# Expert rows in units of 256 instead of 128, with w1 blocks as the stationary operand and gathers three units ahead

## The reference

```python
x = x + attention(layernorm(x), ctx, ctx)      # 16 heads of 16, 154 keys per batch
h = layernorm(x)
top2 = top_k(softmax(h @ router_w.T), 2)       # 8 experts
for e in range(8):
    w   = sum of the token's top2 weights that name e
    out = out + w * (gelu(h @ w1[e].T, exact) @ w2[e].T)   # 256 -> 1024 -> 256
return x + out
```

## Time and profile before

| | us |
|---|---|
| median of 3 runs (505.07 to 507.56) | 507.27 |
| profiled execution, its own time | 507.12 |
| its span in the profile | 505.3 |

### The profile page before, as it was taken

How to read it: one execution, slowest core, us unless ns; L and a number is a source line. 1 busy time by engine, 2 the same in 40 slices (tenths; PEclk the granted TensorE clock), 3 DMA queues, 4 the chain that set the end, 5 groups by cost and what they waited for, 6 DMA issues and landing times.

```text
span 505.3 us, 12174 instructions
## 1 busy us (share of the span) xinstructions
PE 446.7 (88%) x3485; PEld 390.4 (77%) x3486; DVE 332.8 (66%) x792; ACT 233.6 (46%) x403; POOL 250.7 (50%) x301
## 2 busy tenths in 40 slices
PE   7778999999999997227599999999999999999980
PEld 4567888888888885113489999999999889999970
DVE  3678999999999995697357374564436667433440
ACT  2465676766676764220435353442335544333220
POOL 2788877778877775105034244443333436333431
PEclk9799999999999999558979999999999999999986
DMA  8401121111111110601454526244222653222220
GB/s 244 153 0 54 57 81 54 62 52 62 59 76 52 64 53 32 188 2 52 167 188 70 183 44 205 45 127 105 39 42 42 197 198 46 37 42 42 43 35 10
DMA packets 23083, 41.72 MB, mean 83 GB/s; under 512 B 5808, under 2 KB 18736, under 8 KB 22032
## 3 DMA queue, kind: packets, MB, share of 16 engines
q1 hardware_dynamic: 12512, 28.67, 15.9%
q0 software_dynamic: 7056, 9.88, 11.5%
q10 hardware_dynamic: 3488, 2.83, 1.8%
HBM read 25.88 MB, written 9.19 MB: 69 GB/s over the span
## 4 chain that ended last, share of the span: by engine, by line
PE 73%; DVE 8%; DMA 6%; issue 4%; POOL 3%; ACT 2%; ACTq 1%; DVEq 0%; POOLq 0%; SPq 0%
PE ps_s L1223 18%; PE ps_s L1210 17%; PE ps_s L1057 10%; PE ps_t L1240 6%; PE ps_t L1072 6%; DMA big<-in_wexp 3%; PE ps_a L1090 3%; PE ps_c L1107 3%; PE ps_a L1013 2%; PE ps_a L1085 2%; DMA xs<-in_x 2%; PE ps_c L1194 2%; ACT KB L576 2%; PE ps_c L1119 1%; PE ps_c L1113 1%
## 5 line engine op out<-in xcount | busy, mean ns | idle before, releaser
L448 POOL DMA_INDIRECT result<-big,rowtok x36 | 57.1, 1587 | 149.7 <-issue 63.8
L1223 PEld LDWEIGHTS ps_s<-KB,hidT 128*128 128x128 f32 x864 | 108.2, 190 | 5.8 <-issue 2.8
L1210 PE MATMUL ps_s<-KB,xgT 128*128 (+1 forms) x432 | 110.9, 406 | 0.6 <-issue 0.6
L1223 PE MATMUL ps_s<-KB,hidT 128*128 x864 | 109.5, 282 | 2.1 <-issue 2.1
L1210 PEld LDWEIGHTS ps_s<-KB,xgT 128*128 128x128 f32 x432 | 79.6, 191 | 17.5 <-issue 0.8
L602 ACT ACTIVATE hidT<-ps_t 128x512 fp32r<-128x512 f32 x72 | 39.1, 596 | 91.0 <-PE ps_t L1240 91.0
L1057 PE MATMUL ps_s<-KB 128*128 (+1 forms) x384 | 72.2, 324 | 9.6 <-DVE V_all L695 3.2
L584 ACT ACTIVATE big<-ps_s 128x1024 f32<-128x1024 f32 x36 | 36.9, 1026 | 69.1 <-PE ps_s L1210 68.2
L966 DVE TENSOR_TENSOR hidT<-ps_t,hidT 128x512 fp32r<-128x512 f32 x72 | 46.4, 686 | 33.6 <-ACT hidT L602 32.2
L1057 PEld LDWEIGHTS ps_s<-KB 128*128 128x128 f32 x384 | 57.1, 194 | 14.4 <-issue 7.6
L981 DVE TENSOR_SCALAR big<-ps_s,wrow 128x256 f32<-128x256 f32 x36 | 17.4, 483 | 73.3 <-PE ps_s L1223 73.2
(11 more groups left out here) (160 smaller groups left out, 596.3 us busy)
## 6 DMA issues: line engine op xcount, KB each, us to landing
big<-in_wexp SPq DMA_DIRECT2D x8, 2048.0 KB, 7.9
V_cur<-V_all SPq DMA_DIRECT2D x16, 384.0 KB, 2.6
result<-x SPq DMA_DIRECT2D x16, 128.0 KB, 1.7
rows<-xn SPq DMA_DIRECT2D x16, 128.0 KB, 2.1
xs<-in_x ACTq DMA_DIRECT2D x1, 1536.0 KB, 10.8
big<-rows,gtok POOLq DMA_INDIRECT x39
result<-big,rowtok POOLq DMA_INDIRECT x36
big<-in_ctxT SPq DMA_DIRECT2D x1, 308.0 KB, 3.8
```

The costliest lines, as they stand in the source:

```text
L448: pool.indirect_dma_start(out, bass.IndirectOffsetOnAxis(rowtok[:, u:u + 1], 0), ys[:, u % 2, :], None, compute_op=ALU.add).then_inc(added ...
L1210: last = mm(ps_s[0][:, c, :], xgT[:, u % 2, a, k, :], w1[:, bass.ds(par, 1), w, k, 512 * c:512 * (c + 1)].squeeze(1), start=k == 0 and n = ...
L1223: last = mm(ps_s[1][:, u % 2, 0:D], hidT[:, a, j, :], w2[:, bass.ds(par, 1), w, j, :].squeeze(1), start=j == 0 and n == 0, stop=j == HJ - ...
```

## The change

Experts' lists are padded to units (pairs) of 256 rows, at most `PAIRS` = 23, which are two half-units of 128 for gathers and scatters (`SLOTS` is now 46). `up` holds 128x128 blocks of w1 in the array and streams 256 rows, so the hidden layer comes out turned already: the turns L1240 are gone, and `turn` on VectorE makes both its parts from the GELU's output in SBUF. `down` streams high and low part of w2 side by side (512 columns) against the high part of the hidden layer and 256 columns against its low part; the low product lands in the second half of the bank, is scaled on ScalarE (`scale_low`) and added on VectorE. The split w1 is held once, the split w2 twice; they load as two transfers of 1 MB. Gathers go three units ahead, one in front of each of a unit's two scatters. Tests for used units are nested. The two split tables are replaced by four operations in `first_tables`.

```diff
-SLOTS = (2 * TOK + E * (P - 1)) // P
+PAIR = 2 * P
+PAIRS = (2 * TOK + E * (PAIR - 1)) // PAIR
+SLOTS = 2 * PAIRS
@@ ff_pairs
-            for s in range(FF_LOOP, SLOTS):
+            def remaining(s):
                 with if_used(eng, s):
-                    slot(s, s % 4, s // 4, lambda d, s=s: s + d < SLOTS)
+                    pair(s, s % 4, s // 4, lambda d: s + d < PAIRS)
+                    if s + 1 < PAIRS:
+                        remaining(s + 1)
+                    eng.nop()
+            remaining(FF_LOOP)
@@ sync, expert e
-                    sp.wait_ge(w_lo, HALVES * e)
-                sp.dma_start(wraw, wexp[e]).then_inc(w_loaded, 16)
+                    sp.wait_ge(w1_lo, NP1 * e)
+                sp.dma_start(wraw1, wexp[e, :, 0:W1]).then_inc(w1_loaded, 16)
+                if e:
+                    sp.wait_ge(w2_lo, e)
+                sp.dma_start(wraw2, wexp[e, :, W1:WB]).then_inc(w2_loaded, 16)
@@ gpsimd (left_by(s) waits for gtok_made s+2, xgT_made s+1, wrow_made s+1)
+            def pair(s, u, i, has):
+                if has(3):
+                    left_by(s + 1)
+                for h in range(2):
+                    if has(3):
+                        gather((u + 3) % 4, h)
+                    wait_alone(ys_made, 2 * s + h + 1)
+                    if h or not isinstance(s, int) or s >= 1:
+                        wait_alone(added, 32 * s + 16 * h)
+                    pool.indirect_dma_start(out, bass.IndirectOffsetOnAxis(rowtok[:, u, h:h + 1], 0),
+                                            ys[:, 2 * (u % 2) + h, :], None, compute_op=ALU.add).then_inc(added, 16)
                 if isinstance(s, int) and s >= FF_LOOP:
-                    pool.wait_ge(added, 16 * (s + 1))
+                    pool.wait_ge(added, 32 * (s + 1))
@@ scalar
+            def gelu(s):
+                for b in range(4):
+                    act.wait_ge(up_psum, 4 * s + b + 1)
...
+                    act.activation(hid[:, b, :], ps_s[b // 2][:, b % 2, :], ACT.Gelu).then_inc(hid_made, 1)
+            def scale_low(s, u, h):
+                act.wait_ge(down_psum, 2 * s + h + 1)
...
+                act.activation(y_low[:, h, :], ps_t[h][:, D:2 * D], ACT.Copy,
+                               scale=wrow[:, u, h, 3:4]).then_inc(low_made, 1)
+            def pair(s, u, i, has):
+                if has(1):
...
+                    with act.If(to_split >= E):
+                        split_w2(e, e % 2)
+                    with if_used(act, s + 1):
+                        gelu(s + 1)
+                    with act.If(to_split % E > 0):
+                        split_w1(to_split % E)
+                for h in range(2):
+                    scale_low(s, u, h)
@@ vector
+            def turn(s, u):
...
+                for b in range(4):
+                    js = slice(2 * b, 2 * b + 2)
+                    src = hid[:, b, :].rearrange("p (j n) -> p j n", j=2)
+                    dve.wait_ge(hid_made, 4 * s + b + 1)
+                    dve.tensor_copy(hidT[u % 2][:, 0, js, :], src).then_inc(hidT_hi, 1)
+                    dve.wait_ge(hidT_hi, 4 * s + b + 1)
+                    dve.tensor_tensor(hidT[u % 2][:, 1, js, :], src, hidT[u % 2][:, 0, js, :].bitcast(fp32),
+                                      ALU.subtract).then_inc(hidT_lo, 1)
             take_rows(0, 0, True)
             take_rows(1, 1, True)
-            split_tables_2()
-            split_weights(0, 0, 1)
+            split_w2(0, 0)
...
+            turn(0, 0)
+            with dve.If(to_split > 0):
+                split_w1(to_split % E)
+            def pair(s, u, i, has):
...        # as on scalar: split_w2, turn(s + 1), split_w1
+                if has(2):
+                    take_rows(s + 2, (u + 2) % 4, has(4))
+                for h in range(2):
+                    dve.wait_ge(low_made, 2 * s + h + 1)
+                    if not isinstance(s, int) or s >= 2:
+                        dve.wait_ge(added, 32 * (s - 2) + 16 * (h + 1))
+                    dve.scalar_tensor_tensor(ys[:, 2 * (u % 2) + h, :], ps_t[h][:, 0:D], wrow[:, u, h, 3:4],
+                                             y_low[:, h, :], ALU.mult, ALU.add).then_inc(ys_made, 1)
@@ tensor
+            def up(s, u, e):
+                pe.wait_ge(xgT_made, s + 1)
+                for j in range(HJ):
+                    if j % 4 == 0:
+                        pe.wait_ge(w1_lo, NP1 * e + 2 * (j // 4) + 2)
...
+                    for k in range(KC):
+                        for n, (a, w) in enumerate(PARTS):
+                            last = mm(ps_s[j // 4][:, j // 2 % 2, (j % 2) * PAIR:(j % 2 + 1) * PAIR],
+                                      w1[:, w, k, j * P:(j + 1) * P], xgT[:, u % 2, a, k, :],
...
+            def down(s, u, e):
...
+                for h in range(2):
...
+                    for j in range(HJ):
+                        if h == 0 and j % 2 == 0:
+                            pe.wait_ge(hidT_lo, 4 * s + j // 2 + 1)
+                        mm(ps_t[h][:, :].rearrange("p (w d) -> p w d", w=2), hidT[u % 2][:, 0, j, half_rows],
+                           w2[:, bass.ds(par, 1), :, j, :].squeeze(1), start=j == 0, stop=j == HJ - 1,
...
+                        last = mm(ps_t[h][:, 0:D], hidT[u % 2][:, 1, j, half_rows],
+                                  w2[:, bass.ds(par, 1), 0, j, :].squeeze(1), start=False, stop=j == HJ - 1,
...
             row_transposes(0, 0)
-            row_transposes(1, 1)
             pe.wait_ge(pairs_made, 1)
             read_used(pe)
             up(0, 0, 0)
+            row_transposes(1, 1)
+            def pair(s, u, i, has):
...
+                if has(1):
+                    with if_used(pe, s + 1):
+                        up(s + 1, (u + 1) % 4, e1)
+                if has(2):
+                    row_transposes(s + 2, (u + 2) % 4)
+                down(s, u, e0)
```

More of the change, by code:

```diff
@@ L589, in _ @@
             act.activation(r_e2[:, 0:1], lane_sb[:, :], ACT.Gelu)
+            split_w2(0, 0)
             act.wait_ge(pairs_made, 1)
             read_used(act)
+            to_split = act.value_load(table(t_split, 0), min_val=0, max_val=E * E - 1)
             gelu(0)
-            act.wait_ge(tables_made, 1)
-            def slot(s, u, i, has):
+            with act.If(to_split > 0):
+                split_w1(to_split % E)
+            def pair(s, u, i, has):
                 if has(1):
[L597 to L610, removed]
-                            split_weights(e, e % 2, 1)
@@ L616, in _ @@
+            ff_pairs(act, pair)
         @block.vector
@@ L929, in _, with columns @@
-            split_tables_1()
-            def column(a, s):
-                return a[:, s:s + 1] if isinstance(s, int) else a[:, bass.ds(s, 1)]
+            then(dve.tensor_scalar(t_k[:, :, 0], code, 0.0, None, ALU.is_gt))
+            then(dve.tensor_scalar(t_k[:, :, 1], code, 0.0, None, ALU.is_lt))
+            split_w1(0)
+            def columns(a, s):
+                return a[:, 2 * s:2 * s + 2] if isinstance(s, int) else a[:, bass.ds(2 * s, 2)]
             def take_rows(s, u, more):
@@ L988, in _ @@
+            ff_pairs(dve, pair)
         @block.tensor
@@ L1204, in up @@
                 pe.wait_ge(xgT_made, s + 1)
[L1205 to L1207 removed]
+                for j in range(HJ):
+                    if j % 4 == 0:
+                        pe.wait_ge(w1_lo, NP1 * e + 2 * (j // 4) + 2)
+                    if j % 2 == 0 and (not isinstance(s, int) or s >= 1):
+                        pe.wait_ge(hid_made, 4 * s + j // 2 - 3)
                     for k in range(KC):
@@ L1233, in _ @@
             up(0, 0, 0)
-            def slot(s, u, i, has):
-                pair = pe.value_load(table(t_pair, s), min_val=0, max_val=E * E - 1)
-                e0, e1 = pair % E, pair // E
-                pe.wait_ge(hid_made, s + 1)
-                for j in range(HJ):
-                    last = pe.transpose(ps_t[j // 4][:, (j % 4) * P:(j % 4 + 1) * P], hid[:, j * P:(j + 1) * P],
-                                        id_sb[:, :])
-                last.then_inc(hidT_psum, 1)
-                if has(2):
-                    row_transposes(s + 2, (u + 2) % 4)
+            row_transposes(1, 1)
+            def pair(s, u, i, has):
+                both = pe.value_load(table(t_pair, s), min_val=0, max_val=E * E - 1)
+                e0, e1 = both % E, both // E
                 if has(1):
```

304 lines of the change are left out of this document (141 added, 163 removed).

## The result

| | before | changed |
|---|---|---|
| median of 10 runs, us | 506.25 (505.07 to 507.67) | 503.38 (499.91 to 506.35) |
| profiled execution, us | 507.12 | 504.29 |
| its span, us | 505.3 | 502.1 |
| start of up(0) to end of the last down, us | 257.8 | 251.8 |
| start of the last scatter to the end of the span, us | 11.0 | 8.0 |

The ratio is 0.9935, 95% interval 0.9911 to 0.9959: 0.65% faster. 494.5 us had been forecast. The direction was right and the mechanism on TensorE too; three quarters of the gain were missing. All times and ratios are of executions in the chip's usual state; one execution each of the kernels of experiments 9 and 10 was in a slower one (623.87 and 558.91 us) and is not counted.

What follows compares the result with a forecast made beforehand. TensorE was taken to bound the expert stage: pair 0 ends at 268.1, the rest adds 205.3, then 5 for short experts and 4.6 at the end give 483.0; with the tail, 494.5 us, range 488 to 501.

Steps and rivals of the forecast that it cites:

- TensorE per unit: Expert stage: up 5.66, down 5.62 and row turns 0.44 make 11.72 us per unit, against 13.44 for two slots.
- Rival D: TensorE pays 0.190 us for each w1 block in up: +66 us, 560 in all; chance 0.02.
- Units: The experts' lists make 19 units of 256 rows, 38 half-units against 36 slots; padding costs 5.6%.
- The start: VectorE's work in series is late after up(0): up(1) starts near 254.3, pair 0 ends near 268.1.
- VectorE at the short experts: Pairs 10 and 11: 13.8 us of VectorE work, 2.0 too much, and late w1 reloads; 5 us taken.
- The step that failed: GpSimd: two scatters take 9.5 of 11.7 us a unit, hidden; a late one is caught up.
- rival B: Scatters become the bound through GpSimd's chain, from a period of 5.86 us; at 6.5, 517 us; chance 0.09.
- The end: Last down near 483.0; scatter (18,1) may start at 486.3 and lands near 491.
- The skip: Before the last down, skipping up(19) costs a pause of 2.1 us; 2.8 taken because of a gather.
- The credit for nested tests: After the last landing, one skip of 2.1 us (bounds 0 and 6.2) replaces three unused slots' 6.2 us.
- The sum: Span 493 with the 1.8 us around it: 494.5 us, 12.6 less than the profiled run.
- The range: The forecast's own range is 488 to 501 us; 8 in 10 lie in 484 to 508.

Runs made afterwards that it cites:

- experiments 9 and 10: 9: experiment 1, experiment 4 and experiment 5 together, 489.35 us, ratio 0.9650; 10: that plus the hidden layer's cast on ScalarE, 486.87 us, ratio 0.9630.
- experiment 7: Changed kernel with the number of used units one higher, so a 20th unit of padding is worked through: 515.08 us, ratio 1.0170 to the kernel before.
- experiment 4: Changed kernel with VectorE doing split_w2(0) and turn(0) before take_rows(1) at the start: 499.08 us, ratio 0.9835 to the kernel before.
- experiment 1: Changed kernel with both gathers of a unit issued ahead of both scatters: 497.21 us, ratio 0.9783 to the kernel before.
- experiment 2: Changed kernel with each gather moved below its scatter: 604.14 us, ratio 1.195 to the kernel before.
- experiment 5: Changed kernel with gathers, row turns and making of rows' parts skipped for unused units from unit 16 on: 501.23 us, ratio 0.9879 to the kernel before.
- experiment 6: Changed kernel with the tests for used units flat again instead of nested: 503.68 us, ratio 0.9908 to the kernel before.

## Why the prediction was wrong

- **TensorE per unit** was right: 11.60 us for 11.72. Rival D (a price for each new w1 block) is excluded by the row of 5.62 us for 48 products.
- **Units** were right: 38 scatters; a unit costs 11.9 us (experiment 7).
- **The start** was right in order and size: up(1) at 253.2 (254.3 forecast), pair 0's end at 267.8 (268.1). Only up(0) did not pay for the clock, 5.87 us, and other executions of like kernels did, 7.4. That its idle time was what to fill, experiment 4 showed.
- **VectorE at the short experts** was right in size: 2.0 us too much a pair forecast; a pause of 1.4 us in the changed kernel, 2.15 once the gathers were out of the way, 0.36 with the casts elsewhere. Pairs 10 and 11 cost 8.5 us over two undisturbed units, however (up(11) to up(13), 374.6 to 406.4), and 5 had been taken: 4.11 of them are the next point, and 1.9 the lower clock behind it.
- **The step that failed** is this sentence on the scatters: "the gathers stand three units ahead and the results have four buffers, so a late one is caught up". I had asked whether two scatters of 4.75 us fit in a unit, and they do. I had not asked what stands behind a scatter that waits for its results. The gather of rows for three units on is issued behind the first scatter, which in a slow pair starts only when VectorE is through with splits, hidden layer and rows. "Three units ahead" says which rows it fetches, not how long before their use: 391.90 to 398.46 is no slack at all, and it met the second thing that the sentence passes over: beside a weight load a gather too is slow, 6.52 us for 2.8 to 3.1. Experiment 1 took the gathers from behind the scatter, and the slow landing was then hidden; it got 1.5% back, 7.7 us of the 8.9 missing (no run kept the order and moved the load); experiment 2 closed the ring for both gathers and lost 20%. The rival B named GpSimd's chain, but with a wrong price and threshold: a period of scatters over 5.86 us never was the question.
- **The end**: last down at 489.2, 483.0 forecast; 5.7 us of that come from the middle. The pause ahead of the last down was 3.67 (2.8 forecast): the gather that it waited for was issued at 478.77, behind the scatter of 476.88, and the gather before that at 475.60, when the scatter of 469.40 had landed. The last scatter started 4.9 us behind the last down, 3.3 had been forecast. The difference is the distance of the last two, 6.3 us where 4.75 had been taken. A gather for a unit that doesn't exist stands between them, and without it they are 4.6 us apart (experiment 5). But 476.88 and 481.50 have a gather between them too and are 4.6 apart, so the gather alone doesn't explain it, and the cause of the slow landing (5.48 us for 3.8) is open.
- **The skip** was wrongly read. I took the 2.1 us before the last down of the kernel before for the price of skipping an up. They are a wait for the hidden layer: its rounded copy and its remainder are made while the next up runs, and where there is no next up TensorE waits for them (L1223 is down; compare).

```profile
486.62 1.08 ACT L602 ACTIVATE hidT<-ps_t 128x512 fp32r<-128x512 f32 x2 [2.68 <-PE ps_t L1240]
487.25 1.29 DVE L966 TENSOR_TENSOR hidT<-ps_t,hidT 128x512 fp32r<-128x512 f32 x2 [1.02 <-ACT hidT L602]
...
488.89 4.63 PE L1223 MATMUL ps_s<-KB,hidT 128*128 x24 [2.10 <-issue]
```

  The remainder is ready at 488.5, and 0.35 us are left for the skip and all else. The changed kernel paused at this place too, 3.67 us, but for a gather; without that gather (experiment 5) it doesn't pause. That a pause of 2.8 had been forecast there was luck.
- **The credit for nested tests** was wrong for the same reason. The 6.2 us between the last landing and the end before were not three skips: GpSimd's drain alone takes 6.20 of them there. The end did get 3 us shorter, as forecast, but by luck: 2.6 of the 3.0 are the drain, 3.63 us in the changed kernel, and experiment 6 shows that nesting gives 0.6 at most. By the same run the rule of the Trainium skill ("Runtime: NRT & Kernel Launch", § Instruction fetch mechanics) is not borne out here as a price of 2.1 us for each skip.
- **The sum** came out a little low: (18,1) at 486.3, 4.75 to land, 2.1 and 1.8 give about 494.9, not 494.5.
- **The range**: 484 to 508 held the time, in its upper part; the forecast's own, 488 to 501, did not. The forecast took every pause but one as independent of the others. Two of the pauses (short experts, last down) and the six small ones had one cause in common, a gather behind a scatter.

What stays open: what sets GpSimd's drain. The time from the last scatter to the end is 7.9 to 8.6 us in the kernels whose last gather stands at most 10.2 us ahead of the drain (drain 3.6 to 4.1 us), and 10.5 to 11.0 in the kernel before, where it stands 14.2 us ahead, and in the three that skip unused units, where it is earlier still (drain 6.2 to 6.3). No run tells what makes the difference.

## What to carry to other kernels

A prefetch is as early as the instruction that stands in front of it in its queue lets it be; how many units ahead its data lie does not say when it starts. So place it ahead of whatever waits for results, and look for rings: where a wait in one engine's order leads back, over two others, to itself, a delay is paid in every round. Where a start is bound by one engine's work in series, changing its order only moves the pause; filling that engine's idle time, and first doing what releases a load, shortens it. Before a pause is priced as a mechanism of the chip, look for what the next instruction needs and when that was made.

## What the runs showed of the hardware

- An indirect scatter that adds into DRAM lands 3.8 us after its start in the usual case, and the next, which waits for that, starts 4.6 to 4.75 us after it, without a gather between them (experiment 5) or with one (476.88 to 481.50 of the changed kernel). Beside weight loads the next starts 9.1 us after it (388.76 to 397.85 of experiment 1, where its issue was long too). At the end of the changed kernel two scatters (469.40 and 487.81) took 5.3 and 5.5 us to land with no weight load near; that is not explained.
- An indirect gather of 128 rows landed 2.7 to 3.2 us after its start, and 6.5 us beside a weight load (391.90 of the changed kernel).
- A scatter's issue on GpSimd, 1.6 to 2.1 us in most places, took 3.73 at 388.76 in experiment 1 and 3.33 at 410.39 in the changed kernel. Both started inside a VectorE subtraction of 2.29 us with both inputs in SBUF (388.71 to 391.00, and 409.94 to 412.23) and ended 1.5 us behind its end. That is what the prediction had read from the gather of 417.79, but it had priced it by the subtractions of 0.69 us, 0.7 at most, and left out those of `split_w2`.
- A cast of 512 float32 elements from SBUF took 0.43 us on VectorE, as worked out from 308 elements; 0.69 was the subtraction.
- After like pauses of 1.5 us the same up took 5.87 us in one execution (granted clock 1.00) and 7.46 in another (0.77, experiment 4).
- GpSimd's last instruction, a drain, took 3.6 to 4.1 us in eight kernels and 6.2 to 6.3 in four. It is the last thing that all the others wait for.
